# A fused four-layer kernel: column scores taken from a copied row by one-row transposes, with the instruction orders changed around them

## The reference

```
x = x + diffusion(x)                       # neighbours in both directions, and r*x*(1-x)
x = x + pooled(x)                          # below
x = x + x @ W[subject].T + b[subject]
x = x + LN(x + up(relu(down(x))))          # adapter with a bottleneck of 128, layer norm
```

```
attn_in = tanh(hidden @ W1 + b1)                       # 1024 x 128
scores  = attn_in @ v                                  # one number per position
masked_scores = where(mask, scores[None, :], -1e30)    # prefix, postfix or all but itself
p = softmax(masked_scores); pooled = (p @ hidden) / cnt
```

## Time and profile before

| | |
|---|---|
| Time, median of 3 runs | 551.24 us (550.38 to 553.79) |
| The profiled execution | 550.72 us, span of its instructions 548.9 us |
| PE busy | 525.4 us, 96% of the span |
| DVE busy | 478.4 us, 87% |
| ACT and POOL busy | 312.7 us and 313.5 us, 57% each |
| Chain that ended last | PE 81%, DVE 11%, ACT 3%, issue 3%, POOL 1% |
| Granted TensorE clock, mean | 0.998 of full speed |
| Transfers | 100.82 MB, mean 184 GB/s |

### The profile page before, as it was taken

One profiled execution on the slowest core, in us unless ns is written; L12 is line 12 of the kernel. 1 busy time (PEld: TensorE's weight loads), 2 busy tenths in 40 slices (PEclk: granted clock), 3 DMA queues, 4 the chain that ended last, 5 costly groups with the idle time before them and its releaser, 6 DMA issues.

```text
span 548.9 us, 8952 instructions
## 1 busy us (share of the span) xinstructions
PE 525.4 (96%) x2793; PEld 411.0 (75%) x2793; DVE 478.4 (87%) x1197; ACT 312.7 (57%) x546; POOL 313.5 (57%) x283
## 2 busy tenths in 40 slices
PE   8997899999999999999999999999999999999995
PEld 3556677888588877888678885888778886888783
DVE  6659788999899997999899998999979998887677
ACT  5645564477536765567645775376654776344520
POOL 5146826596258935687275952589256872247231
PEclk9999999999999999999999999999999999999999
DMA  7984199567996599884997579974997856422652
GB/s 251 304 203 78 59 308 257 108 140 165 347 232 135 100 260 314 195 168 98 309 301 162 121 183 345 225 142 89 274 348 147 164 107 207 59 59 57 132 87 109
DMA packets 63941, 100.82 MB, mean 184 GB/s; under 512 B 10893, under 2 KB 16525, under 8 KB 63894
## 3 DMA queue, kind: packets, MB, share of 16 engines
q0 software_dynamic: 16544, 29.90, 33.2%
q1 hardware_dynamic: 38096, 53.54, 30.8%
q10 hardware_dynamic: 9254, 16.81, 8.1%
HBM read 67.43 MB, written 31.98 MB: 181 GB/s over the span
## 4 chain that ended last, share of the span: by engine, by line
PE 81%; DVE 11%; ACT 3%; issue 3%; POOL 1%; DVEq 0%; ACTq 0%; POOLq 0%
PE y L711 38%; PE front_ps L774 9%; PE front_ps L872 8%; PE front_ps L711 6%; PE front_ps L798 5%; PE front_ps L727 4%; PE front_ps L782 3%; PE front_ps L788 2%; DVE x2f L1628 2%; PE front_ps L819 2%; ACT zh L1192 2%; DVE pn L1575 1%; PE front_ps L846 1%; PE y L753 1%; PE front_ps L853 1%
## 5 line engine op out<-in xcount | busy, mean ns | idle before, releaser
L597 POOL TENSOR_TENSOR norm<-norm 128x1 f32<-128x1 f32 x64 | 51.3, 802 | 150.5 <-DVE norm L1655 149.6
L711 PE MATMUL y<-wth,x2h 128*128 128x512 f32 x256 | 103.9, 406 | 0.0
L711 PE MATMUL y<-wth,x2l 128*128 128x512 f32 x256 | 100.2, 392 | 0.0
L711 PE MATMUL y<-wtl,x2h 128*128 128x512 f32 x256 | 100.0, 390 | 0.0
L615 POOL TENSOR_TENSOR x2l<-x2f,x2h 128x1024 fp32r<-128x1024 f32 x32 | 76.9, 2404 | 15.1 <-ACT x2h L1063 14.4
L578 POOL TENSOR_TENSOR xd<-xn 128x1024 f32<-128x1024 f32 x28 | 55.7, 1989 | 36.1 <-DVE x L1484 19.8
L1628 DVE SCALAR_TENSOR_TENSOR x2f<-alb,small,front_ps 128x128 f32<-128x128 f32 x256 | 70.6, 343 | 1.3
L872 PE MATMUL front_ps<-th_pt,x 128*128 128x129 f32 x512 | 64.8, 278 | 2.7 <-DVE x2f L1628 1.8
L872 PEld LDWEIGHTS front_ps<-th_pt,x 128*128 128x128 f32 x512 | 62.0, 190 | 7.0 <-DVE x2f L1628 4.8
L604 POOL DMA_DIRECT2D out<-o_sb x58 | 57.6, 1072 | 8.0 <-ACT o_sb L1209 7.0
L1063 ACT ACTIVATE x2h<-x2f 128x1024 fp32r<-128x1024 f32 x32 | 34.0, 1062 | 47.1 <-DVE x2f L1628 47.1
(11 more groups left out here) (146 smaller groups left out, 1094.4 us busy)
## 6 DMA issues: line engine op xcount, KB each, us to landing
xn<-in_x SPq DMA_DIRECT2D x32, 512.0 KB, 7.7
out<-x ACTq DMA_DIRECT2D x58, 256.0 KB, 4.4
out<-o_sb POOLq DMA_DIRECT2D x58, 256.0 KB, 6.5
xu<-in_x SPq DMA_DIRECT2D x21, 512.0 KB, 8.9
xu<-in_x POOLq DMA_DIRECT2D x21, 512.0 KB, 8.0
wn_wd<-in_L_cond_weight SPq DMA_DIRECT2D x8, 1024.0 KB, 7.7
wn_wd<-in_L_cond_down_w SPq DMA_DIRECT2D x8, 256.0 KB, 6.9
up_row<-in_L_cond_up_b SPq DMA_DIRECT2D x8, 256.0 KB, 4.6
```

Of the source, the lines that this page charges most:

```text
L597: pool.tensor_tensor(rstd[:, r:r + 1], ve[:, r:r + 1], minus_half[:, :], ALU.pow).then_inc(rstd_ready, 1)
L711: ins = mm(dst, lhs, rhs, start=first and q == 0, stop=last and q == len(parts) - 1, skip_group_check=True)
```

## The change

The column scores are no longer computed. ScalarE copies partition 0 of the spread scores, 1 x 512 for each half, into partition 0 of `th` (a new step `keep_scores`, with a new semaphore `score_kept`); it does so after VectorE has read that half. TensorE then makes the column scores by eight transposes of 1 x 128 pieces of that row, each one instruction with one column moving. `th` in partition 0 is overwritten, which both uses of `th` before have left behind by then.

```
+            def keep_scores(n, h):
+                act.wait_ge(sb_read, 2 * n + h + 1)
+                copy(th[0:1, half(h)], pair_b[0:1, half(h)]).then_inc(score_kept, 1)

             def scores_by_row(n):
-                pe.wait_ge(th_ready, 2 * n + 2)
+                pe.wait_ge(score_kept, 2 * n + 2)
                 for j in range(NJ):
-                    ins = mm(SN[:, j:j + 1], th[:, blk(j)], v_col[:, :], start=True, stop=True)
+                    ins = pe.transpose(SN[:, j:j + 1], th[0:1, blk(j)], ident[0:1, 0:1])
                 ins.then_inc(sn_ps, 1)
...
                     spread_scores(m, 1)
+                linear(n, q, 2)
+                if m is not None:
                     scores_by_row(m)
-                linear(n, q, 2)
-                if m is not None:
+                    down_through_w(m)
                     block_sums(m)
-                    down_through_w(m)
                 linear(n, q, 3)
+                adapter_up(n, q, 2)
                 if m is not None:
                     transpose_p(m, 0)
-                adapter_up(n, q, 2)
```

More of the change, by code:

```diff
@@ L247, in build @@
         sn_ps = sem("sn_ps")
+        score_kept = sem("score_kept")
         sb_read = sem("sb_read")
@@ L642, in steady @@
             def steady(b, n, m, q):
+                finish(b, 0)
+                root(b, 1)
                 if m is not None:
@@ L647, in steady @@
                     add_below(m, 1)
-                root(b, 1)
-                finish(b, 0)
+                    add_below(m, 2)
+                rest_up(n, q)
+                root(b, 2)
                 if m is not None:
                     left_and_right(m, 1)
-                rest_up(n, q)
-                root(b, 2)
+                start_sum(n)
                 rest_difference(n)
-                if m is not None:
-                    add_below(m, 2)
-                start_sum(n)
+                finish(b, 2)
                 root(b, 3)
+                rest_x2(n, q, 0)
                 finish(b, 1)
-                rest_x2(n, q, 0)
                 if m is not None:
                     add_below(m, 3)
-                finish(b, 2)
-                root(b, 4)
                 rest_x2(n, q, 1)
@@ L668, in steady @@
                 rest_x2(n, q, 2)
+                root(b, 4)
                 root(b, 5)
@@ L672, in steady @@
                 finish(b, 5)
+                root(b, 6)
                 finish(b, 4)
@@ L675, in steady @@
                     left_and_right(m, 3)
-                root(b, 6)
+                finish(b, 6)
                 root(b, 7)
                 root(n, 0)
-                finish(b, 6)
                 finish(b, 7)
@@ L1761, in steady @@
                 maxima(n)
+                keep_x3(b, 2)
                 moments(b, 1)
+                subtract_mean(b, 1 - q, 1)
+                adapter_bias(n)
                 block_weights(n)
-                subtract_mean(b, 1 - q, 1)
-                keep_x3(b, 2)
                 row_weights(n)
-                adapter_bias(n)
+                probabilities(n, 0)
                 rest_v(n)
-                probabilities(n, 0)
                 probabilities(n, 1)
@@ L1809, in steady @@
                     add_around(m, 1)
+                subtract_mean(b, 1 - q, 5)
+                keep_x3(b, 7)
+                moments(b, 6)
                 rest_w(n, 0)
-                keep_x3(b, 7)
-                subtract_mean(b, 1 - q, 5)
                 if m is not None:
                     times_x(m, 1)
-                moments(b, 6)
-                if m is not None:
-                    add_around(m, 2)
                 subtract_mean(b, 1 - q, 6)
```

191 lines of the change are left out of this document (99 added, 92 removed).

## The result

| | before | after |
|---|---|---|
| Median of 6 runs | 551.31 us (550.38 to 553.79) | 585.6 us (585.5 to 587.02) |
| Ratio | | 1.062, interval 1.060 to 1.064 |
| The profiled execution | 550.72, span 548.9 | 585.51, span 583.7 |
| Mean granted clock | 0.998 | 0.970 |

What follows compares the result with a forecast made beforehand. TensorE was taken to bound the kernel, busy 62.68 of a 63.74 us turn. Seven batches -5.8, six gaps -3.6 and the first batch +1.2 made -8.2 from 550.72: 542.5 us, range 538.6 to 548.6.

Steps and rivals of the forecast that it cites:

- The x2 loop: VectorE's loop ahead of transpose_w: 1.2 us to spare, some 0.5 us left after the change, so costed at nothing.
- the third rival: VectorE's two-input x2 steps meet GpSimd steps, up to 2.4 us each; 0.8 a turn back, 548.1 us; chance 0.27.
- The prediction's own last sign of being wrong: On VectorE: a step of 1.2 us that shows 2 or 3 would show the forecast wrong.
- The chain to the probabilities: VectorE's steps up to transpose_p: L1572 takes 0.17 to 0.6 us, TensorE's gap shrinks from 0.83 to 0.2.
- The column scores: On TensorE: 1.68 us a batch removed, eight transposes at 0.85 added; 0.83 saved a batch, 1.24 at best.
- the bound of 0.44: Lower end for the eight transposes on TensorE, in us, if transposes' 50 ns shorter loads are half of a load's time.
- the second rival: Cheap loads on TensorE: a one-column transpose costs 0.055 us, 7 x 0.41 more saved, 539.6 us; chance 0.10.
- TensorE's turn: Length of a steady turn on TensorE: 62.3 us after the change, where it was 63.74.
- The first batch: Batch 0, paced by VectorE and ScalarE: exps and probabilities about 0.8 us later; +1.2 us, between 0 and 2.5.
- The copies: Two 1 x 512 ScalarE activations, about 0.59 us each, done 0.65 us before TensorE arrives: hidden.
- the fourth rival: TensorE waits for score_kept, the copy 2.7 us or more late; 558.6 us at 3.0 late; chance 0.07.

Runs made afterwards that it cites:

- both moves: Kernel after with GpSimd's root of tile 4 ahead of the second rest_x2 and rest_up behind rest_difference; 550.76 us, ratio 0.998 to the kernel before.
- GpSimd's old orders: Kernel after with all three GpSimd lists of the kernel before; 549.31 us, ratio 0.997 to the kernel before; measured again 549.11, ratio 0.9956.
- the run with `rest_x2` first: Kernel after with the second rest_x2 ahead of the fourth add_below's transfer issues, root of tile 4 unmoved; 560.38 us, ratio 1.018 to the kernel before.

## Why the prediction was wrong

**The x2 loop** is the step that failed. It was costed "at nothing" because every step there took its own time before, and 0.5 us seemed to be left. The mechanism that breaks it is the one of the third rival, on a pair that it named (`diffuse` on a `rest_x2`; TensorE then waits not at `transpose_w` but at `adapter_up`, for the `keep_x3` behind `diffuse`). But it was given at most 2.4 us, a mean of 1.3 less the 0.5, and 27% in a range that closed at 549.5. The hold measured 4.2 to 4.8 us in each of six turns (`diffuse` at 5.46 to 5.99). Two things were missed. The list of GpSimd was read only at the start of the turn: that `root` 4 moves from ahead of the second `rest_x2` to behind the third is part of the change and stands in no sentence of the prediction. And the price was taken from one GpSimd instruction, while the hold also took in the issues ahead of it. (The upper end of the range, 548.6, is called the middle of this rival; the middle of 545.5 to 549.5 is 547.5. The result is far above either.) The prediction's own last sign of being wrong, a VectorE step of 1.2 us that shows 2 or 3, is there with 5.99.

The Trainium skill, "SBUF — State Buffer", section "SBUF: two separate sides", says that whichever of the two starts first has the shared ports for the whole instruction. The trace agrees where one step meets one step (1.7 us, until the end of `rest_x2`). It disagrees with "whole instruction" as an upper bound: 4.8 us over issues and a tensor step, and L1470 held over three steps. Nor did the first win in after: `diffuse` is recorded from 324.45, `rest_x2` from 325.38, and `diffuse` was held. The measurement decides.

**TensorE's clock** was in no term. In the turn from 295.02, which is 5.36 us longer than before's, 4.42 are standing still (5.25 against 0.83, from the timelines). The rest is work that takes 63.9 us against 62.5 at full clock in the same orders of TensorE: 1.3 us, lost while the clock was 0.50 (less the 0.4 saved, that makes the 0.94 left). A large product there starts every 0.43 us instead of 0.23. Over the six turns, 24.8 of the 35.4 us are standing still (29.6 against 4.8). The other 10.6, and the 2.4 that the new order saves at full clock (0.4 a turn), were lost in nine such stretches of low clock, about 1.4 us each. Six of them follow the wait that `diffuse` causes, one in each turn. Three follow the wait ahead of `transpose_p`; the turns with these take 70.2 to 70.4 us, and the others 68.7 to 69.1.

**The chain to the probabilities.** L1572 was to take 0.17 to 0.6 and takes 0.29: right. That the gap shrinks to 0.2 is wrong: it grew to 1.96. `rest_up`, which was to be out of the way behind "transfer issues", now stood in the queue when the next small step and the probabilities came, which the prediction gave their old durations; both were held. With `rest_up` elsewhere (both moves) they have them, and the gap is gone in most turns. So the sum of that step was right for a kernel without the meeting.

**The column scores** were mis-sized, on the good side: 0.58 for eight, not 0.85; the bound of 0.44 was nearer, and the second rival came nearly true (1.10 saved a batch, where it had 1.24). The Trainium skill, "TensorE: Matmul & The Clock Gate", section "LDWEIGHTS (loading the stationary operand)", has the load depend on the columns and not on the rows, which by its formula made 0.85, an estimate by that page. The trace disagrees for the pace: one starts every 72 ns, each recorded load takes 136 ns, and they overlap.

**TensorE's turn** was to be 62.3. Without the two meetings it is 63.0 to 63.2. Summed from start to start, TensorE's work is 62.92 in a turn of before and 62.52 in one of the kernel with GpSimd's old orders: 0.4 less, where 0.83 was taken and the scores alone give 1.1. The matmuls of L711 take 34.9 us there against 34.2. Of these 0.7, 0.4 only change their place: the first of them behind the spread scores takes 0.63 us to the next start, and the spread scores themselves 1.56 instead of 1.96. The other 0.3, and 0.4 in the transposes, `pool_blocks` and the small products, are small pieces; which of them belong to the new order no run tells (TensorE changes from one line to another 30 times a turn in both kernels). To that come 0.66 of waiting (0.46 of it at `transpose_w`, which is VectorE in the x2 loop), where 0.2 were forecast.

**The first batch.** Forecast +1.2. From the first spread scores to those of batch 1 it is 52.71 us in after as in before, and with GpSimd's old orders 54.25. So +1.2 was too much for after and near for the version without the meetings. Its terms are not shown: with both moves, where GpSimd's list for that part is the one of after, it is 54.28. For GpSimd's old orders this 1.5, and 3.4 saved in six turns of 0.57 each, make 549.4 from 551.3; 549.3 is measured.

**The copies and the fourth rival.** The copies take 0.59 and are done 0.5 us ahead of TensorE, against the 0.65 forecast. Only in batch 0 does it wait for them, 0.9. The large loss thus came by the third mechanism and not by the one to which the losing side had been given.

**What stays open.** In after, `diffuse` is recorded from 324.45 and `rest_x2` only from 325.38, and VectorE was still held. In the same way L1577 was held and let go before `rest_up` is recorded. Issues alone don't hold such a step: L1477 in the kernel before takes 1.22 beside four of them, and the step of L1577 takes 0.17 beside three, with `rest_up` ahead of them or moved well behind (there at the same distance from the first issue as in after, 0.38 us). The recorded starts are rough too: behind issues `rest_x2` is recorded for 3.97 us instead of 2.40 and `rest_up` for 2.86 instead of 1.28, both beginning while the last issue still runs. Whether the tensor step behind the issues holds VectorE before its recorded start, or VectorE's start is recorded early, no run here tells. What stands behind the issues decides whether VectorE is held; that is shown. How it is held is not.

## What to carry over

When an edit shifts two engines against each other, list for each VectorE step with two inputs in SBUF what GpSimd has in its queue at that time, before and after, over the whole turn and not only around the edit; a small GpSimd step that waits for VectorE, placed between the transfer issues and a large one, decides who goes first. Price such a meeting by the end of the whole unbroken run of GpSimd work, and add what TensorE's clock loses behind a gap of some microseconds. A saving on the bottleneck engine of 1 us in a turn of 64 is no larger than one of these meetings, so the order has to be searched again for the new durations and measured, and not only predicted.

## What the runs showed of the hardware

- Eight one-row fp32 transposes (one partition, one column moving) take 0.58 us, 72 ns each; a full fp32 transpose of 128 x 128 takes 109 ns in the same kernel (0.87 for eight).
- A 1.2 us VectorE step with two SBUF inputs took 5.1 to 6.3 us beside GpSimd work without a break; a 0.17 us one took 3.45.
- Where one step met one step, the one that had started first ran through: a root of 0.55 us on GpSimd, recorded 0.11 us behind `diffuse`, took 1.54, and `diffuse`, 0.49 us behind a `rest_x2` in the run with `rest_x2` first, took 2.94. A `rest_x2` queued behind transfer issues held a `diffuse` recorded 0.93 us ahead of it.
- Behind a gap of 3.03 us on TensorE the granted clock was 0.50, its lower level, from 333.2 to 336.4, and the turn lost 1.3 us by it. Behind the wait ahead of `transpose_p` (1.96 to 2.19 us) it fell in three turns of after and not in the other three.
